# A latent cross-attention stage rewritten: queries for two sequences at once, output projection in seven row tiles, straight code

## The reference, cut to what matters

```python
z = layernorm(x[b])                               # 112 x 1024
rows = concat(ctx_4096[b], z)                     # 375 + 112 = 487 rows
k, v = rows @ Wk.T, rows @ Wv.T                   # 487 x 384 each
q = z @ Wq.T                                      # 112 x 1536
p = softmax(q_h @ k_g.T / sqrt(96))               # 16 heads, four heads to a group g
x[b] = x[b] + tanh(g_xattn[0]) * (concat_h(p @ v_g) @ Wo.T)
```

## Time and profile before

| what | us |
|---|---|
| median of 3 runs | 2917.91 (2915.89 to 2923.22) |
| profiled execution, own time | 2914.22 |
| its span, first to last instruction | 2912.5 |
| the latent stage's TensorE work | 18.41 to about 953.6 |
| time between the starts of two sequences | 116.6 |
| granted TensorE clock, mean of the span | 0.953 |

### The profile page before, as it was taken

One profiled execution on the slowest core, in us unless ns is written; L12 is line 12 of the kernel. 1 busy time (PEld: TensorE's weight loads), 2 busy tenths in 40 slices (PEclk: granted clock), 3 DMA queues, 4 the chain that ended last, 5 costly groups with the idle time before them and its releaser, 6 DMA issues. The chain is left out here.

```text
span 2912.5 us, 50231 instructions
## 1 busy us (share of the span) xinstructions
PE 2643.2 (91%) x18888; PEld 1847.6 (63%) x18892; DVE 1883.6 (65%) x3362; ACT 1069.3 (37%) x2474; POOL 566.3 (19%) x610
## 2 busy tenths in 40 slices
PE   7999999999999479998988899998878999878898
PEld 4665766756657168786745565555567878656664
DVE  5546446455463676776566777777647988966774
ACT  3433433334333333232324444443435556312222
POOL 0100101101001210000024444444313332300000
PEclk9999999999999789999988999998889999988999
DMA  7110101101100665453554456554160001434421
GB/s 266 45 40 14 36 13 50 36 13 44 41 8 1 243 176 147 138 131 111 203 209 140 143 173 174 174 166 145 44 221 14 24 23 45 124 124 177 177 94 39
DMA packets 153764, 304.69 MB, mean 105 GB/s; under 512 B 83936, under 2 KB 107136, under 8 KB 144056
## 3 DMA queue, kind: packets, MB, share of 16 engines
q1 hardware_dynamic: 127064, 229.90, 24.2%
q0 software_dynamic: 19376, 57.15, 6.7%
q10 hardware_dynamic: 7120, 15.01, 1.8%
HBM read 246.39 MB, written 43.04 MB: 99 GB/s over the span
## 5 line engine op out<-in xcount | busy, mean ns | idle before, releaser
L1588 DVE TENSOR_REDUCE latent_nmax<-bank 112x1 f32<-112x487 f32 x128 | 85.2, 666 | 245.1 <-PE bank L1453 237.5
L2262 PE MATMUL bank<-ffn_qT,gather_whole 128*128 128x128 bf16 x3584 | 209.4, 221 | 16.3 <-ACT ffn_us L2385 5.9
L2262 PEld LDWEIGHTS bank<-ffn_qT,gather_whole 128*128 128x128 fp8e4 x3584 | 205.6, 99 | 21.1 <-issue 19.9
L2002 POOL TENSOR_SCALAR grouped_probs<-grouped_probs,grouped_rsum 112x375 f32<-112x375 f32 x256 | 159.8, 642 | 292.7 <-DVE grouped_rsum L2057 292.4
L1376 POOL TENSOR_SCALAR latent_probs<-latent_probs,latent_rsum 112x487 f32<-112x487 f32 x128 | 87.8, 686 | 636.7 <-DVE latent_rsum L1593 636.7
L2445 POOL TENSOR_TENSOR ffn_h<-ffn_sl,ffn_us 128x512 f32<-128x512 f32 x56 | 128.0, 2287 | 277.4 <-ACTq L2388 277.4
L1413 PEld LDWEIGHTS bank<-latent_hT,latent_wq 128*128 128x128 f32 x1536 | 175.3, 192 | 7.3 <-issue 7.1
L1949 ACT ACTIVATE grouped_probs<-bank,grouped_nmax 112x375 f32<-112x375 f32 x256 | 143.1, 572 | 94.0 <-DVE grouped_nmax L2053 94.0
L2053 DVE TENSOR_REDUCE grouped_nmax<-bank 112x1 f32<-112x375 f32 x256 | 122.3, 540 | 82.4 <-PE bank L1860 79.8
L1413 PE MATMUL bank<-latent_hT,latent_wq 128*128 128x112 f32 x1536 | 175.1, 275 | 0.0
L1391 PE MATMUL bank<-latent_wv,latent_hT 128*125 128x384 f32 (+1 forms) x512 | 167.9, 489 | 0.0
(11 more groups left out here) (419 smaller groups left out, 5412.0 us busy)
## 6 DMA issues: line engine op xcount, KB each, us to landing
grouped_raw<-L_weights SPq DMA_DIRECT2D x24, 2048.0 KB, 8.6
points_spread<-numbers SPq DMA_DIRECT2D x16, 912.0 KB
codes<-grouped_flip SPq DMA_DIRECT2D x24, 512.0 KB, 2.6
latent_hT<-ctxT SPq DMA_DIRECT2D x8, 1500.0 KB
plain_ctxT<-ctxT POOLq DMA_DIRECT2D x8, 1500.0 KB
plain_ctx<-ctx POOLq DMA_DIRECT2D x8, 1500.0 KB
grouped_ctx<-ctxT SPq DMA_DIRECT2D x8, 1500.0 KB, 6.7
gather_whole<-numbers SPq DMA_DIRECT2D x12, 912.0 KB
```

Of the source, the lines that this page charges most:

```text
L2002: pool.tensor_scalar(pr[:, g % 2, j, :], pr[:, g % 2, j, :], rsum[:, g % 2, j:j + 1], 1.0, ALU.mult, ALU.mult)\
L2262: mm = pe.matmul(ahead.tile(t)[:, i * P:(i + 1) * P], wgu[:, u0 + f // 4, c:c + 2 * P - 1:2], qT[:, k, :], start=(k == 0), stop=(k == KC - 1))
```

## The change

Only `latent_attention` changes, and one figure of the program: the space that GpSimd's DMA descriptors are written to is halved (8192 to 4096), as the new buffers take its place.

- No hardware loops: all eight sequences are written out.
- Sequences go in pairs. In an even one, the next one's rows z are transposed too, and `latent_keys` and `queries` stream the rows of both (224 columns). Six query groups of two chunks: 0 to 2 ahead of the even sequence's heads, 3 to 5 at its steps 1, 3 and 5. The odd sequence has no queries of its own: its queries wait in a second `qT`, its rows' keys in `kL`.
- Keys: the context's 375 columns for each sequence, and the z rows' keys once per pair.
- An odd sequence does its keys first and its values behind them, right ahead of the scores.
- Output projection: the rows of all sequences are cut into seven tiles of 128. Tile b-1 is projected at the end of sequence b (none at the end of sequence 0). `outputs` on ScalarE therefore writes into two tiles of `oT`, which are cut at column 16b; it takes up to eight instructions for a group where there were four.
- Result: VectorE adds gate times bank to x itself (`result`); ScalarE's and GpSimd's parts of that are gone.
- z has one buffer, loaded by SP. For an even b, `load_z(b + 1)` stands behind the store of tile b-2 and the load of tile b-1; VectorE norms it (`normal(b + 1)`) ahead of sorts 2 to 4, and the square root for it stands on ScalarE behind the third value copy. For an odd sequence, three sorts are done at the end of the even one.

```diff
-        qT = wide[0:HD, 0:H * Q].rearrange("p (h q) -> p h q", h=H)
+        qT = [wide[0:HD, 0:H * Q].rearrange("p (h q) -> p h q", h=H), s_.sb("qT", [HD, H, Q])[:]]
-        oT = s_.sb("oT", [P, OC, Q])
+        oT = s_.sb("oT", [P, 2, OC, P])
...
+            load_z(0)
+            load_rest(0)
+            load_x(0)
+            for b in range(B):
+                if b >= 2:
+                    store_x(b - 2)
+                    load_x(b - 1)
+                if b + 1 < B:
+                    load_z(b + 1)
                     load_rest(b + 1)
...
+            def latent_keys(b):
+                pe.wait_ge(zT_ready, b + 2)
+                for i in range(3):
+                    t = ("kL", b, i // 2)
+                    if i % 2 == 0:
+                        pe.wait_ge(turns.free(t), turns.count(t, 0))
+                    for k in range(KC):
+                        mm = pe.matmul(turns.tile(t)[:, i % 2 * 2 * Q:(i % 2 + 1) * 2 * Q], wk[:, k, i * P:(i + 1) * P],
+                                       zT[:, k].rearrange("p s q -> p (s q)"), start=(k == 0), stop=(k == KC - 1))
+                    if i >= 1:
+                        mm.then_inc(turns.full(t), 1)
+
+            def queries(b, i):
...
+                for c in range(2):
+                    for k in range(KC):
+                        mm = pe.matmul(turns.tile(t)[:, c * 2 * Q:(c + 1) * 2 * Q], wq[:, k, (2 * i + c) * P:(2 * i + c + 1) * P],
+                                       zT[:, k].rearrange("p s q -> p (s q)"), start=(k == 0), stop=(k == KC - 1))
+                mm.then_inc(turns.full(t), 1)
...
+            for b in range(B):
+                if b % 2 == 0:
+                    latents(b)
+                    for i in range(4):
+                        values(b, i)
+                    keys(b)
+                    latents(b + 1)
+                    latent_keys(b)
+                    for i in range(3):
+                        queries(b, i)
+                else:
+                    keys(b)
+                    for i in range(4):
+                        values(b, i)
                 pe.wait_ge(kT_ready, b + 1)
...
-                projected(0)
-                projected(1)
-                outputs(2 * KV - 1)
-                projected(2)
-                projected(3)
+                if b >= 1:
+                    projected(b, 0)
+                    projected(b, 1)
+                outputs(b, 2 * KV - 1)
+                if b >= 1:
+                    projected(b, 2)
+                    projected(b, 3)
...
+            def outputs(b, g):
...
+                for n, to, c in ((b - 1, slice(P - ahead, P), slice(0, ahead)), (b, slice(0, Q - ahead), slice(ahead, Q))):
+                    if 0 <= n < TILES and c.start < c.stop:
+                        act.activation(oT[0:HD, n % 2, 3 * g:3 * g + 3, to], src[0:HD, 0:3, c], ACT.Copy)
+                        for j in range(3):
+                            op = act.activation(oT[HD:P, n % 2, 3 * g + j, to], src[j * (P - HD):(j + 1) * (P - HD), 3, c], ACT.Copy)
...
+            for b in range(B):
+                if b % 2 == 0:
+                    copy_turned(act, turns, zT[:, :, 0, :], "zT", b, 0, zT_ready)
+                    values(b, 0)
+                    squares(b, 2)
+                    values(b, 1)
+                    values(b, 2)
+                    norm.root(act, 0, b + 1)
+                    squares(b, 3)
+                    values(b, 3)
+                    keys(b, 0)
+                    squares(b, 4)
+                    keys(b, 1)
+                    keys(b, 2)
+                    copy_turned(act, turns, zT[:, :, 1, :], "zT", b + 1, 0, zT_ready)
+                    latent_keys(b)
+                    act.wait_ge(points.sq_free, b * 5 + 7)
...
+            def result(b):
+                dve.wait_ge(x_loaded, 16 * b)
                 for i in range(2):
...
+                    dve.scalar_tensor_tensor(out=x[:, c], in0=turns.tile(t)[:], scalar=C.gates[:, gate:gate + 1], in1=x[:, c],
+                                             op0=ALU.mult, op1=ALU.add).then_inc(turns.free(t), 1)
...
+            for b in range(B):
+                if b % 2 == 0:
+                    normal(b + 1)
+                for i in range(2 + b % 2, 5):
+                    sort(b, i)
...
+                if b + 1 < B:
+                    if b % 2 == 1:
+                        normal(b + 1)
+                    points.begin(dve, b + 1, 0, b + 1)
+                    for i in range(2 if b % 2 == 1 else 3):
+                        sort(b + 1, i)
+                if b >= 1:
+                    result(b)
...
-    nc = bacc.Bacc("TRN2", target_bir_lowering=False, num_devices=1, dynamic_dma_scratch_size=8192)
+    nc = bacc.Bacc("TRN2", target_bir_lowering=False, num_devices=1, dynamic_dma_scratch_size=4096)
```

More of the change, by code:

```diff
@@ L1385, in _, with fill @@
             pe.wait_ge(wv_loaded, 16)
-            def fill(t, b, lhsT, rhs, m, n, chunks):
-                pe.wait_ge(turns.free(t), turns.count(t, b))
-                for k in range(chunks):
-                    mm = pe.matmul(turns.tile(t)[0:m, 0:n], lhsT(k), rhs(k), start=(k == 0), stop=(k == chunks - 1))
+            def fill(t, lhsT, rhs, m, n):
+                pe.wait_ge(turns.free(t), turns.count(t, 0))
+                for k in range(KC):
+                    mm = pe.matmul(turns.tile(t)[0:m, 0:n], lhsT(k), rhs(k), start=(k == 0), stop=(k == KC - 1))
@@ new lines, in outputs @@
+            def outputs(b, i):
+                g, half = i // 2, i % 2
+                t = ("o", b, g)
+                pe.wait_ge(pT_ready, b * H + (2 * i + 2))
+                if half == 0:
+                    pe.wait_ge(turns.free(t), turns.count(t, 0))
+                for k, (c, n) in enumerate(KT):
+                    mm = pe.matmul(turns.tile(t)[0:HD, 2 * half * Q:2 * (half + 1) * Q], v[0:n, k, g * HD:(g + 1) * HD],
+                                   pT[0:n, half, k], start=(k == 0), stop=(k == len(KT) - 1))
+                mm.then_inc(turns.full(t) if half else half_done, 1)
@@ new lines, in projected @@
+            def projected(b, g):
+                pe.wait_ge(wo_loaded, 16)
+                pe.wait_ge(oT_ready, b * KV + (g + 1))
+                for i in range(2):
+                    t = ("y", b, i)
+                    if g == 0:
+                        pe.wait_ge(turns.free(t), turns.count(t, 0))
+                    for k in range(3 * g, 3 * g + 3):
+                        mm = pe.matmul(turns.tile(t)[:], oT[:, (b - 1) % 2, k, :], wo[:, k, i * 512:(i + 1) * 512],
+                                       start=(k == 0), stop=(k == OC - 1))
+                    if g == KV - 1:
+                        mm.then_inc(turns.full(t), 1)
@@ new lines, in _ @@
+                squares(0, i)
+            for b in range(B):
+                if b % 2 == 0:
[14 more added lines that the diff above has]
+                    act.wait_ge(points.sq_free, b * 5 + 7)
+                    for i in range(3):
+                        queries(b, i)
+                else:
+                    act.activation(kT[:, :, CTX:S], kL[:], ACT.Copy)
+                    for i in range(3):
+                        keys(b, i)
+                        if i < 2:
+                            squares(b, 3 + i)
+                    act.drain().then_inc(kT_ready, 1)
+                    for i in range(4):
+                        values(b, i)
@@ L1554, in sequence @@
-                outputs(KV - 1)
-                if not last:
-                    points.squares(act, b + 1, 0, 1, (5 * (1 - s) + 1) % 2)
-                for i in range(2):
-                    empty(("y", i), y[:, i * 512:(i + 1) * 512], turns.tile(("y", i))[0:Q, :],
-                          scale=C.gates[0:Q, gate:gate + 1])
-                act.drain().then_inc(y_ready, 1)
-            every(act, sequence)
+                outputs(b, KV - 2)
+                if b + 1 < B:
+                    if b % 2 == 1:
+                        norm.root(act, 0, b + 1)
+                    squares(b + 1, 0)
```

322 lines of the change are left out of this document (146 added, 176 removed).

## The result

Before, the median is 2920.3 us in the runs beside the changed kernel; changed, it is 2888.18 (2887.75 to 2890.45). The ratio is 0.9896, with the interval 0.9881 to 0.9911: 26 to 35 us faster. The forecast was 2892. The profiled execution took 2890.45, its span is 2888.5.

What follows compares the result with a forecast made beforehand. TensorE bounds the latent stage (116.28 of 117 us busy). Savings of 48.8 less gaps of 22.6 give 26.2 off 2914.22, 2888.0; plus 3.7 for the median, 2892. Range for 8 in 10 runs: 2873 to 2907.

Steps and rivals of the forecast that it cites:

- (b): First pair: sorts and the norming of z(1) hold ScalarE back, so TensorE waits for z copies; 3.5 us lost.
- (c): Odd sequences' first heads, without queries to overlap: waits at the third score and at scores 4 and 5; 4.8 us lost.
- (d): Sequence 0's end without projection, 1.2 us, and sequence 1's maxima queued behind sorts, 5.0; together 6.2 us lost.
- Queries, projection, end: Latent stage savings: 26.0 us from paired queries, 20.6 from seven tiles not eight, 2.4 from VectorE's add at the end.
- The rival that the pairing does not pay: Queries and rows' keys: 224 columns cost two of 112, 0.223 us a record; kernel slower at 2924; chance 0.02.
- Loops: Latent stage loops written out: ScalarE's 2.80 us idle times at loop turns lie beside TensorE's work; zero gain.
- Keys: Latent stage keys: context at 0.315 us a record, the pair's z rows at 0.189; 157.3 against 157.1, 0.2 lost.
- (a): Even sequences: second z transposes stand right ahead of matmuls needing ScalarE's copies; 1.5 us lost, three pairs, 4.5.
- what the prediction set beside its sum: TensorE idling at sequence 1's wait may return at its 1.2 GHz level: 2.2 us once, 2894; chance 0.2.
- (e): Heads: output copies cut into eight instructions delay the next exponential; 0.3 us lost twelve times, 3.6.
- Few gaps: Rival for the latent stage: most gaps close to their lower bounds, about 6 us in all; 2876; chance 0.20.
- The late z(b+1): Rival: z(b+1) arrives late, holding up VectorE's sorts and maxima and ScalarE's query copies; 20 us late gives 2928; chance 0.04.

Runs made afterwards that it cites:

- the first repetition: The changed kernel run again with nothing edited: 2888.63 us, the stage's last store issued at 926.99.
- four such edits: Changed kernel plus odd sequences' last value tile behind two scores, earlier second z transposes, 256-column head ring, sequence 1's first sort earlier: 2868.46 us, ratio 0.9824.

## Why the prediction was right

The work taken out was right to within a microsecond, and so was the kind of every gap. The sizes of (b), (c) and (d) were not, and two losses to the clock were left out of the sum; that the total came out within a microsecond is in part luck.

- **Queries, projection, end:** 26.0, 20.6 and 2.4, as forecast. The rival that the pairing does not pay is out: 0.189 and not 0.223.
- **Loops:** taken at zero, and zero they are. But the idle times of ScalarE were misread: at its loop's two turns and its end it sat idle for 3.00, 2.80 and 0.25 us, not three times for 2.80. At most 6 us were at stake and not 8.
- **Keys:** 1.0 lost, not 0.2. The context's records are 0.316, not 0.315, and z's 0.191, not 0.189; small, and within the two prices that were given.
- **(a)** 1.5 each in three pairs, with ScalarE's copy as releaser: 4.5 as forecast.
- **(b)** 2.5 us (the transposes at 56.78 and 0.77 long, the keys at 60.09), not 3.5: the copies were ready at 60.1 and not at 61.5, of which 0.7 is the first sort's earlier start (27.83, in the earlier trace rows 28.49). But the 48 key records behind it take 10.95 and not 9.35, 1.6 more, at a granted clock of 0.72, which has no term in the sum. Together 4.1, in the execution shown; in the first repetition it was the wait alone, 2.9.
- **(c)** 0.98 and 0.52 at an odd sequence's third and fifth scores, 1.5 as forecast. This term's error is the largest. What was missed is that queries now stand at steps 1, 3 and 5 of even sequences, so the 0.48 that both kinds of sequence lost before at the fifth score is gone in the even ones as well: some 2.2 in all, not 4.8.
- **(d)** At sequence 0's end 1.05, forecast 1.2. In sequence 1 the wait costs 3.6 over an odd sequence's own, not 5.0, and the clock another 2.2: from the first score to the projection sequence 1 takes 216.71 - 176.92 = 39.79, sequence 3 takes 447.15 - 413.18 = 33.97, and 5.8 is 3.6 and 2.2. In the first repetition it is 38.40, and the clock's part 0.8. The 2.2 is what the prediction set beside its sum, read from the idle start. The Trainium skill (TensorE: Matmul & The Clock Gate, HAM oscillation) has it that an idle gap that is long enough throttles the array anew. The traces agree at this gap of 4.4 us: behind it the clock fell in all seven profiles that have it, and at this place in none of the three without it. The prediction gave this a chance and not a place in its sum. It named (d) as the only place; the first pair's dip is a second.
- **(e)** Twelve times 0.35 is 4.2, forecast 3.6.

In sum: 48.0 and 0.45 for an earlier start, less 4.5 + 4.1 + 2.2 + 1.05 + 3.6 + 2.2 + 4.2 = 21.9, is 26.6, against 26.85 measured. The closeness to the forecast's 26.2 is luck: waits of (b), (c) and (d) counted 1.0, 2.6 and 1.5 too high, 5.1 in all, stand against 3.8 of clock that was left out, 0.8 too little for the keys and 0.6 for (e), and 0.45 of start. Few gaps (2876) was wrong in this kernel but right as to what ScalarE's and VectorE's order can do: the same work in another order, with the same engines, brought 2868. The late z(b+1) is out as well: TensorE waits nowhere in the stage for longer than 1.4 us but at (b) and (d).

The medians differ by 32, and the stage by 26 to 30. The rest is within the scatter of what follows the stage; no step explains it, and none is claimed.

## What to carry to other kernels

An fp32 matmul of 112 columns here costs what the load of its 128 weight columns costs: widen the moving side until the columns set the pace, and take the price from a stage that has that width already. Work that is taken off the bounding engine was also somebody's cover: before counting it, ask which engine's queue ran beside it, and move that queue's work first. Small waits at fixed places of a sequence are each worth an edit of order; here four such edits gave 20 us at the stage's end, beside the 26 to 30 of the change itself. And divide the stage before giving a gain to an edit: some of what an edited kernel gained here lay in a part that the edit didn't touch.

## What the runs showed of the hardware

- Behind sequence 1's wait of 4.4 us the granted clock was lower in all seven executions that had it, and back at 1.00 within 10 us of the wait's end. What it cost differed between executions of one kernel, 0.8 to 2.2 us. The first pair's wait of 2.2 to 2.8 us was followed by a dip in two of four (0.72 over 6 us behind 2.38 and 2.61, but 1.00 behind 2.76 and 2.17). There was none behind this stage's waits of 0.8 to 1.6.
- 128 columns of fp32 weights and 112 streamed took 0.1115 to 0.1117 a record, 224 took 0.189, 375 took 0.316 and 487 took 0.409: 2.0 cycles a column at the 2.4 GHz level, but for the 112. With 112 weight columns and one streamed it was 0.094.
- The program behind the stage took 1948 to 1968 us in these kernels though it was the same code. A change of a few microseconds is read from the stage, not from the total, and best from the part of it that repeats: 654.4 to 654.5 us in three executions.
